# Three score banks with side bank 1 as a place in their ring, score products first in every tile, gelus over two banks

## The reference

```python
h = tok(x, W)                                   # patches of 16, real FFT, matmul -> (16, 1024, 64)
# layer 0
qkv = layernorm(h) @ qkv_w.T + qkv_b            # 8 heads of 8 channels
attn = softmax(q @ k.T * 8 ** -0.5 + bias[i % 7, j % 7]) @ v
h = h + attn @ proj_w.T + proj_b
f = layernorm(h)
a = relu(f @ Wi.T + bi)
for l in range(2):
    a = relu(a @ Ws[l].T + bs[l] + a @ Wr[l, route].T + br[l, route] + a)
h = h + a @ Wo.T + bo
# layer 1
h = h + attention(layernorm(h))                 # no table bias
f = layernorm(h)
mask = one_hot(top_k(f @ Wg + bg, 2)).sum(-2)
y = gelu(einsum('td,edh->teh', f, W1) + b1) @ W2 + b2
h = h + einsum('ted,te->td', y, mask)
```

## Time and profile before

| | |
|---|---|
| runs, median of 3 | 4241.19 us (4240.89 to 4246.01) |
| profiled execution | 4239.35 us, span 4237.5 us, mean granted clock 0.98 |
| TensorE busy | 3920.9 us, 93% |
| VectorE busy | 2902.9 us, 69% |
| ScalarE busy | 2728.1 us, 64% |
| GpSimd busy | 859.5 us, 20% |
| DMA | 156.30 MB, mean 37 GB/s |

### The profile page before, as it was taken

One profiled execution on the slowest core, in us unless ns is written; L12 is line 12 of the kernel. 1 busy time (PEld: TensorE's weight loads), 2 busy tenths in 40 slices (PEclk: granted clock), 3 DMA queues, 4 the chain that ended last, 5 costly groups with the idle time before them and its releaser, 6 DMA issues.

```text
span 4237.5 us, 61596 instructions
## 1 busy us (share of the span) xinstructions
PE 3920.9 (93%) x21509; PEld 1301.7 (31%) x21509; DVE 2902.9 (69%) x4956; ACT 2728.1 (64%) x4896; POOL 859.5 (20%) x1263
## 2 busy tenths in 40 slices
PE   5988999999999999999999999999999999999796
PEld 3222323233332323323232332323333232332222
DVE  3866757677675766857677675767867677686571
ACT  0555767667676666767667676666767667676474
POOL 4122212121121312212121211312212131220211
PEclk7899999999999999999999999999999999999898
DMA  5213211222122122212222121122211212210100
GB/s 102 36 25 56 37 29 31 41 48 41 29 39 41 31 41 49 38 22 31 52 37 41 35 38 35 31 41 48 41 24 32 53 31 41 42 28 19 31 1 6
DMA packets 115606, 156.30 MB, mean 37 GB/s; under 512 B 21391, under 2 KB 63119, under 8 KB 115261
## 3 DMA queue, kind: packets, MB, share of 16 engines
q1 hardware_dynamic: 115297, 152.36, 20.5%
HBM read 120.01 MB, written 29.36 MB: 35 GB/s over the span
## 4 chain that ended last, share of the span: by engine, by line
PE 66%; ACT 10%; DVE 8%; issue 7%; POOL 3%; DMA 2%; SPq 1%; POOLq 0%; ACTq 0%; DVEq 0%
PE acc L866 17%; PE st L852 17%; PE nat L832 15%; DVE tile_max L1252 5%; PE side L799 3%; ACT hidden L1027 2%; ACT prob L1056 2%; PE side L696 2%; PE side L673 2%; PE side L785 2%; PE side L753 1%; DMA k_rows<-k_scratch 1%; ACT hidden L972 1%; DVE ln_s L1157 1%; POOL centred L1340 1%
## 5 line engine op out<-in xcount | busy, mean ns | idle before, releaser
L1252 DVE TENSOR_REDUCE tile_max<-nat 128x1 f32<-128x512 f32 x4096 | 2598.6, 684 | 1170.3 <-PE nat L832 1150.1
L1056 ACT ACTIVATE prob<-st 128x512 f32<-128x512 f32 x4096 | 2298.1, 596 | 1362.5 <-PE st L852 1309.6
L852 PE MATMUL st<-q_rows,k_rows 99*128 99x512 bf16 x4096 | 1572.8, 384 | 65.2 <-ACT prob L1056 55.7
L832 PE MATMUL nat<-k_rows,q_rows 96*128 96x512 bf16 x4096 | 1449.7, 386 | 88.9 <-DMA k_rows<-k_scratch 41.6
L866 PE MATMUL acc<-prob,v_padded 128*32 128x512 f32 x8192 | 1096.6, 607 | 1.0 <-ACT prob L1056 1.0
L852 PEld LDWEIGHTS st<-q_rows,k_rows 99*128 99x128 bf16 x4096 | 398.3, 97 | 1312.2 <-ACT prob L1056 1030.7
L832 PEld LDWEIGHTS nat<-k_rows,q_rows 96*128 96x128 bf16 x4096 | 402.0, 98 | 629.2 <-DVE tile_max L1252 346.7
L1412 POOL TENSOR_SCALAR max_parts<-neg_max 128x16 bf16<-128x16 f32 x128 | 26.3, 206 | 1685.5 <-DVE neg_max L1259 1205.4
L866 PEld LDWEIGHTS acc<-prob,v_padded 128*32 128x32 f32 x8192 | 161.4, 108 | 338.4 <-issue 276.9
L1337 POOL TENSOR_SCALAR ln_s<-ln_s 128x8 f32<-128x8 f32 x64 | 13.0, 203 | 986.5 <-DVE ln_s L1157 986.5
L799 PE MATMUL side<-hidden,w 128*64 128x512 f32 x512 | 136.5, 616 | 0.0
(11 more groups left out here) (129 smaller groups left out, 2105.8 us busy)
## 6 DMA issues: line engine op xcount, KB each, us to landing
q_rows<-q_scratch SPq DMA_DIRECT2D x288, 128.0 KB
k_rows<-k_scratch SPq DMA_DIRECT2D x96, 384.0 KB
x_rows<-in_x SPq DMA_DIRECT2D x62, 512.0 KB, 6.7
q_scratch<-hidden SPq DMA_DIRECT2D x32, 384.0 KB
k_scratch<-hidden SPq DMA_DIRECT2D x96, 128.0 KB
group_weights<-in_routed SPq DMA_DIRECT2D x64, 129.0 KB, 2.1
q_rows<-max_rows SPq DMA_DIRECT2D x512, 3.0 KB
out_h<-out_rows SPq DMA_DIRECT2D x16, 256.0 KB, 2.1
```

The lines of the kernel that those rows point to most:

```text
L832: eng.matmul(NAT[place % len(NAT)][:, :], QA[u][0:K_NAT, h, c:c + P], KA[u][0:K_NAT, h, kh * 512:kh * 512 + 512], start=True, stop=True)\
L852: eng.matmul(ST[n % 2][:, :], KA[u][0:K_ALL, h, t * P:t * P + P], QA[u][0:K_ALL, h, half * 512:half * 512 + 512], start=True, stop=True)\
L1056: eng.activation(prob[:, n % TILES, :], ST[n % 2][:, :], ACT.Exp).then_inc(exp_done, 1)
L1252: eng.tensor_reduce(mx[:, q % 2, j // 8, j % 8 // 2, j % 2:j % 2 + 1], NAT[place % len(NAT)][:, :], AX.X, ALU.max).then_inc(nat_free, 1)
```

## The change

1. The tensor `side_st` holds four banks: side bank 0, and three banks `RING`. The ring has the two former score banks and the former side bank 1. Which bank a score product or a use of side bank 1 takes is set by `score_ring` at build time: the one taken longest ago. The product waits for what used that bank last (an exp, or the evacuation of a side product). So after a side product before tile n, tile n + 2 gets its bank; elsewhere tile n waits for the exp of tile n - 3, and right after a side product for that of n - 2, as before.
2. The turned maxima (`TN`) are a side stage with side bank 1, at tile 23 of each super tile, where the turn stood. The nat ring has nat products alone. The turn multiplies by 128 columns (48 hold data). `rows_out` follows the tile's reduction, since side stages do. SyncE's `max_dma` waits for the evacuation and stands among the tile's side stages. GpSimd's `split_max` waits for the transfers of two super tiles back. A turn in the first super tile, whose rows nobody read, is gone.
3. The score product precedes the nat product in every tile.
4. Each gelu takes 1024 columns over two neighbouring banks; `fw_ready` and `he_ready` count once for each expert. The last two tiles ahead of FW keep off the ring bank that FW takes first.
5. The experts' outputs add up in side bank 0 instead of 1.

```diff
-TURN = 5
-RING_USES = SUPER + 1
+TURN = 23
...
-    "L1": ((0,), (1,)), "WO": ((0,),), "GATE": ((0, 1),), "MT": ((0,),), "OUT": ((0,),), "FY0": ((1,),),
+    "L1": ((0,), (1,)), "WO": ((0,),), "GATE": ((0, 1),), "MT": ((0,),), "OUT": ((0,),), "FY0": ((0,),), "TN": ((1,),),
...
     put(150, "HO1", r)
+    for q in range(2 * SUPERS):
+        put(SUPER * q + TURN, "TN", q + 1)
...
+def score_ring():
+    tile_bank, tile_prev, side_at, side_prev = {}, {}, [], []
+    last, order = [None] * 3, [0, 1, 2]
+
+    def take(bank, use):
+        prev, last[bank] = last[bank], use
+        order.remove(bank)
+        order.append(bank)
+        return bank, prev
+
+    for kind, _, n0, side in program_phases():
+        steps = {0: side} if kind == "serial" else side
+        for n in sorted(steps):
+            for name, b, k, *_ in steps[n]:
+                if name == "FW":
+                    last[:] = [("hidden", E * b + E - 1), ("hidden", E * b + E), ("hidden", E * b + E)]
+                    order[:] = [0, 1, 2]
+                if name in SIDE_BANKS and 1 in SIDE_BANKS[name][k]:
+                    bank, prev = take(order[0], ("side", len(side_at)))
+                    side_at.append(bank)
+                    side_prev.append(prev)
+            if kind != "serial" and n >= 0:
+                hidden_next = any(x[0] == "FW" for m in (n + 1, n + 2) for x in steps.get(m, ()))
+                free = [bank for bank in order if not (hidden_next and bank == 0)]
+                tile_bank[n0 + n], tile_prev[n0 + n] = take(free[0], ("tile", n0 + n))
+    return tile_bank, tile_prev, side_at, side_prev
...
-        ST = [bank("st0"), bank("st1")]
+        four = ctx.enter_context(nc.psum_tensor("side_st", [P, 2048], F32))
+        side_pair, score_pair = four[:, 0:1024], four[:, 1024:2048]
+        RING = [four[:, 512 * k:512 * k + 512] for k in (1, 2, 3)]
         ACC = bank("acc")
-        SIDE = [bank("side0"), bank("side1")]
+        SIDE = [four[:, 0:512], RING[0]]
...
+            def bank_wait(prev):
+                if prev is not None:
+                    by, value = prev
+                    if by == "tile":
+                        eng.wait_ge(exp_done, value + 1)
+                    elif by == "side":
+                        eng.wait_ge(side_free[1], value + 1)
+                    else:
+                        eng.wait_ge(he_ready, value)
...
+            def turn(n0, q, n):
+                eng.wait_ge(parts_ready, over(n0, SUPER) + q + 1)
+                eng.matmul(side_bank(n, 1)[:, 0:P], mpart[:, q % 2, :], ident_b[:, :], start=True, stop=True)\
+                    .then_inc(side_full[1], 1)
...
-                eng.wait_ge(exp_done, at(n0 + n - 1))
-                hidden_out(side, found, n, 1)
-                hidden_out(side, found, n - 1, 0)
+                bank_wait(TILE_PREV[n0 + n])
...
-                    scores_first = n % HEADS >= 2
-                    if scores_first:
-                        scores(kind, it, n0, n, side, found)
+                    scores(kind, it, n0, n)
                     if kind != "last" or q < SUPERS:
                         nat(kind, it, n0, ahead)
-                    if not scores_first:
-                        scores(kind, it, n0, n, side, found)
...
                 for e in range(E):
-                    both = SIDE if e % 2 == 0 else (ST[slot % 2], ST[(slot + 1) % 2])
-                    for par in range(2):
-                        eng.wait_ge(fw_ready, at(2 * E * b + 2 * e + par + 1))
-                        eng.activation(HE[:, e, par * 512:par * 512 + 512], both[par][:, :], ACT.Gelu,
-                                       bias=b1[:, e:e + 1]).then_inc(he_ready, 1)
+                    both = side_pair if e % 2 == 0 else score_pair
+                    eng.wait_ge(fw_ready, at(E * b + e + 1))
+                    eng.activation(HE[:, e, :], both[:, :], ACT.Gelu, bias=b1[:, e:e + 1]).then_inc(he_ready, 1)
...
+            def rows_out(n0, q, n):
+                v = over(n0, SUPER) + q
+                eng.wait_ge(maxrow_in[q % 2], at(DMA_MAX * (v // 2)))
+                bk = full(n, 1)
+                eng.tensor_copy(mrow[:, q % 2, :], bk[0:PARTS * 4 * HEADS, 0:P]).then_inc(side_free[1], 1)
```

More of the change, by code:

```diff
@@ L218, in program_phases @@
             first[n + 2 * k].append(part)
+    first[-1] = list(side_parts([("TN", 0)]))
+    for q in range(SUPERS):
+        first[SUPER * q + TURN] += side_parts([("TN", q + 1)])
     ending = side_schedule(B - 1, True, False, False)
@@ L230, in program_phases @@
     f1 = side_schedule(B, True, False, False)
-    end += [x for n in sorted(f1) for x in f1[n] if x[0] not in ("SCR", "VC", "RL", "HO1")]
+    end += [x for n in sorted(f1) for x in f1[n] if x[0] not in ("SCR", "VC", "RL", "HO1", "TN")]
     return [
@@ L264 @@
          "CT", "OTR", "ZK", "PROJ", "BO", "H1", "L0", "L1", "WO", "GATE", "RANK", "MT", "OUT", "WCL", "WCA",
[L265 removed]
+         "bank0", "bank1", "FW", "TN"] + [f"FY{k}" for k in range(E + 1)]
 def counted_phases():
@@ L625, in body @@
                     return
[L626 to L635 removed]
+                for n in sorted(side):
+                    for k, stage in enumerate(side[n]):
+                        if stage[0] == "TN":
+                            max_dma(kind, it, stage[1], found[n, k])
+                        else:
+                            side_stage(stage, found[n, k],
+                                       n0 + n if kind == "first" or kind == "pair" and 0 < it < B - 2 else 0)
             run_phases(eng, reg, body)
@@ L1281, in body @@
                     q = ahead // SUPER
-                    if ahead % SUPER == TURN and (kind != "last" or q <= SUPERS):
-                        rows_out(n0, q, last=(kind == "last" and q == SUPERS))
                     if kind != "last" or q < SUPERS:
```

133 lines of the change are left out of this document (56 added, 77 removed).

## The result

The changed kernel takes **4289.78 us** (median of 4 runs, 4281.89 to 4293.21), the kernel before in the same session 4241.11 us: the ratio is **1.011 (95% interval 1.0097 to 1.0123)**, 48.7 us slower. The profiled execution took 4293.21 us for a span of 4291.4 us, 53.9 us more than the span before. The forecast was 4309 us, in a range of 4225 to 4370.

A forecast was written before the change was run, and what follows sets the result against it. TensorE, busy 93% of the span, was taken as the bound, so only its waits counted. Gains and late-bank stalls summed to +4.4 us per pass, +68 over 15.5 passes: 4309 us, 8-in-10 range 4225 to 4370.

The forecast's parts named there:

- Plain cycles: 22 four-tile cycles without side work: leading score products and a third bank give 2.85 instead of 2.93 us, -1.8 per pass.
- Other cycles: Fifteen cycles where score products waited for ScalarE's side work or nat products for VectorE's: 0.02 to 0.5 us each, together -2.5.
- Turned maxima: Turn at tile 23 of 32: cast behind the reduction returns its ring bank late, +4.2 us per pass; backlogged turns +0.34 each.
- gains that GpSimd swallows: Ahead of turns waiting for GpSimd's parts, whose chain stays as long: about 0.9 us of the gains is lost, +0.9.
- Held turns: Three turns per pass that GpSimd holds up: no wait followed before, so each takes the full 0.69 us.
- The transfer behind tile 87: Later cast at tile 87 delays the transfer that the next super tile's first score product awaits: +0.57 us, within the +4.2.
- Other side products: Side bank 1's other users, evacuated behind their tile's reduction or exp, stall score products in six places: +4.7 us per pass.
- Gelus: Experts' gelus merged to 1024 columns: 0.5 us sooner, and 0.59 less wait behind them with a third bank; together -1.1.
- Sum: All terms of one pass: -1.8 - 2.5 + 0.9 + 4.2 + 4.7 - 1.1 = +4.4 us.
- Whole span: The per-pass sum taken over 15.5 passes: +68 us, giving 4307 profiled and 4309 as median.
- The stalls are paid back: Rival, faster: banks return in time or later waits vanish, leaving only gains, -4.5 us per pass, 4171 us; chance 0.15.
- Transfers as the bound: Rival: if maxima transfers take 6.2 us from the cast, five turns stand 0.6 us more, +3.1 per pass, 4357; chance 0.17.

The follow-up runs named there:

- experiment 1: Changed kernel with VectorE casting the turned maxima out of their score bank before the same tile's natural reduction, not behind it: 4213.51 us, 0.9938 of the kernel before.
- experiment 2: Changed kernel with the other side stages on side bank 1 (not QK) emptied before their own tile's reduction or exponential, turned maxima unchanged: 4236.23 us, 0.999.
- experiment 3: Changed kernel with both turned maxima and side stages of side bank 1 emptied before their own tile's reduction or exponential: 4157.07 us, 0.9788.
- experiment 5: Changed kernel with the old order: the natural product leads again in tiles 0 and 1 of four, three score banks kept: 4276.37 us, 1.0079.
- experiment 6: Kernel before with the score product leading in every tile, still two score banks: 4317.76 us, 1.0185.
- experiment 4: Changed kernel with each gelu of 1024 columns split again into two of 512, the second handing on the count: 4291.53 us, 1.012.
- experiment 8: Kernel emptying turned maxima and side stages first (4157 us), with the turn one tile later, 24 of 32: 4244.32 us, 1.0.
- experiment 7: Changed kernel with the natural product of tile 24 of 32 issued three times into the same bank, the last handing over: 4290.01 us, 1.0119.

## Why the prediction was right, and where its sizes were off

The sign, the mechanism and its places were right: banks handed back late hold up TensorE, at the turns and the side stages that it named, and experiments 1 to 3 took the loss back by VectorE's and ScalarE's order alone. By its own steps, per pass:

- *Plain cycles* -1.8: measured -1.6. Seventeen of the 22 fell by 0.08 and one by 0.13; four stayed at 2.91 to 2.93. In three of these (behind tiles 13, 141 and 201) a side product's bank comes back late at a place where the prediction counted 1.9 us as enough. The projection's, at tile 141:

```profile
1950.84 0.69 DVE L1281 TENSOR_REDUCE tile_max<-nat 128x1 f32<-128x512 f32 x1 [0.76 <-PE nat L877]
1951.45 0.74 DVE L1221 TENSOR_TENSOR h0c<-side_st,h0c 128x256 f32<-128x256 f32 x2
...
1952.25 0.39 PE L889 MATMUL side_st<-q_rows,k_rows 99*128 99x512 bf16 x1
```

VectorE is done with the bank at 1952.19, and the score product goes 0.06 later, 0.52 behind the one before it and not 0.44. Emptied first (experiment 2), these cycles take 2.85. The step gave the gain to the order, naming the bank beside it; experiments 5 and 6 show that it takes both.
- *Other cycles* -2.5: measured -2.9.
- *Turned maxima* +4.2, with +0.9 for gains that GpSimd swallows, 5.1: measured 3.8. Held turns 3 x 0.81 (forecast 3 x 0.99), plain ones 2 x 0.35 (0.43; the turned product now holds TensorE 0.06 and not 0.17), those with backlog 0.57 and 0.43 (0.34 each). Experiment 1 took all of it back in sum by VectorE's order alone.
- *The transfer behind tile 87* +0.57: measured -0.37, **the term that failed**. It assumed that the transfer lands a fixed time after its cast. SyncE's queue, before and then after:

```profile
1860.31 1.39 SPq L490 DMA_DIRECT2D x_rows<-in_x  x2
1862.22 0.27 DVE L1243 CAST max_rows<-nat 48x128 bf16<-48x128 f32 x1
```
```profile
1892.65 1.39 SPq L529 DMA_DIRECT2D x_rows<-in_x  x2
1895.16 0.27 DVE L1274 CAST max_rows<-side_st 48x128 bf16<-48x128 f32 x1
...
1901.09 0.39 PE L889 MATMUL side_st<-q_rows,k_rows 99*128 99x512 bf16 x1 [0.17 <-DMA q_rows<-max_rows]
```

The first of the two transfers of x rows went out 1.91 us ahead of the cast before and 2.51 ahead of it after, and the first score product followed it by 8.5 and 8.4 us: the wait follows the large transfer ahead, not the cast. So it does in the other runs: from the last transfer of the x rows to the score product it is 7.2 to 7.7 us in all fourteen traces, by medians, and from the cast 5.5 to 6.5. That is why the turn and the wait behind it take 10.3 to 10.4 us together in every column of the table.
- *Other side products* +4.7: measured 4.6 (1.25, 1.16, 1.17, 0.93, 0.17, -0.05).
- *Gelus* -1.1: measured -1.35, 0.70 in the cycle with the gelus (forecast 0.5) and 0.66 behind it (0.6). One gelu of 1024 columns lasts 1.11 us, but the next begins 1.01 to 1.08 after it, as the 1.02 had it, and the loop takes 2.55 (2.56).
- *Sum* +4.4, measured +2.6: 1.3 of the difference are the turns with their transfer, 0.4 the other cycles, 0.3 the gelus, and 0.2 the other way the plain cycles. The clock, which the prediction did not foresee, added 0.7 again.
- *Whole span* +68, measured +53.9 in the trace. That it came so near is in part luck: some 9 us of it are the six halved stretches and 6.6 are the start, where experiment 4's trace, of the same kernel up to there, is that much shorter. Without the two some 38 are left.
- *Rivals.* "The stalls are paid back" fell: the stalls stand in the cycles at the sizes worked out, 1.25 for 1.23 and 1.16 for 1.16 at CT, or at four fifths of them, 0.81 for 0.99 at the held turns. What it said of the gains is confirmed, since with the stalls mostly gone (experiment 3) 4157 stands where it said 4171. Transfers as the bound: no wait of that kind came at the five turns it named, and experiment 8 shows where it would have. The 6.2 us that the prediction set as the transfer's upper bound was at least 1.5 too many.

## What to carry to other kernels

When buffers of one ring are shared between a fast and a slow user, look first at where the slow user's evacuation stands in its engine's order: here one and the same change lost 49 us with the evacuations behind the tile's own work, and gained 84 with them ahead of it. On an in-order engine, work that waits for nothing goes ahead of work that may wait, and only there: the right order is chosen tile by tile, not once. And a small transfer's landing is read from what lies ahead of it in its queue, not from its own start.

## What the runs showed of the hardware

**The clock halved behind two waits of TensorE close together, but not each time.** Windows of the changed kernel's trace (length; busy time and count of PE, PEld, DVE, ACT, POOL; granted clock; DMA share; GB/s): two neighbouring passes, and a stretch within the first.

```profile
2091.07:2347.66 256.59, 238.85 (x1329) 79.14 (x1328) 180.40 (x308) 163.91 (x299) 51.95 (x78) 0.99 0.21 37
2347.66:2602.92 255.26, 237.51 (x1333) 79.09 (x1336) 180.59 (x309) 164.11 (x300) 51.97 (x78) 1.00 0.21 38
2213.00:2217.50 4.50, 2.89 (x13) 0.70 (x15) 3.29 (x7) 2.28 (x4) 3.08 (x7) 0.83 0.69 91
2217.50:2221.00 3.50, 3.50 (x19) 0.79 (x11) 1.56 (x4) 1.45 (x3) 3.08 (x3) 0.73 0.16 39
```
```profile
2214.44 0.23 PE L863 MATMUL side_st<-ident_b,max_parts 128*128 128x128 bf16 x1 [1.07 <-POOL max_parts L1448]
...
2216.08 0.61 PE L889 MATMUL side_st<-q_rows,k_rows 99*128 99x512 bf16 x1 [0.54 <-DVE max_rows L1274]
2216.48 0.63 PE L877 MATMUL nat<-k_rows,q_rows 96*128 96x512 bf16 x1
2217.04 1.94 PE L903 MATMUL acc<-prob,v_padded 128*32 128x512 f32 x8
```

TensorE stood still 1.07 us for GpSimd's parts and soon after 0.54 for the cast; then 0.61 for a product of 512 columns instead of 0.38, and 1.94 for acc instead of 1.06, is the lower of the two levels (1.2 GHz and not 2.4), for some 3.4 us. Such a pass is some 1.5 us longer. Four of the changed kernel's six such stretches stand behind a turn of this kind (at 2216, 2728, 3353 and 3752 us). The other two (at 912 and 1424) stand behind the q/k and the v product, whose banks are late too:

```profile
906.94 0.39 PE L889 MATMUL side_st<-q_rows,k_rows 99*128 99x512 bf16 x1 [1.37 <-ACT hidden L1006]
...
912.10 0.58 PE L889 MATMUL side_st<-q_rows,k_rows 99*128 99x512 bf16 x1 [1.10 <-DVE v_natural L1197]
```

The kernel before ran at 1.00 in every eighth of all thirteen passes; its held turns have the first wait (0.86 us) and no second. So did experiments 3 and 5, in which the second wait is gone or shorter (0.40 and not 0.54 behind a held turn), and experiment 1, which keeps the two waits at the q/k and v products. Experiment 2 had eight such stretches, all behind the turn at tile 23; experiment 7 one, behind the v product; experiment 4, with all the waits of the changed kernel, none. With transfers of 1.1 to 3.2 us to wait for (experiment 8) the clock fell in all thirteen passes. So such waits went ahead of every halving in these passes but do not suffice for one; what decides between passes stays open. It may also explain in part why the changed kernel's runs spread over 11 us: the two slower of the four have a mean granted clock of 0.976, the two faster 0.978.
